# Cross-attention on array tiles: scores in 64x64 tiles over four banks, attention in 128x32 column tiles in one bank

## Chip, core and metric

The kernel runs on one core of one Trainium2 chip, in one launch. The metric is the device time of an execution in microseconds; the median of three executions before the change is 878.66 us (877.78 to 878.94).

## What is computed

One perceiver block over 32 sequences of 32 tokens, 512 wide, in three parts. Cut to what matters:

```
x = x + xattn(layernorm(x), ctx, ctx, mask)       # 16 heads of 32, 257 context rows per sequence
    Q = query @ Wq.T + bq;  K = key @ Wk.T + bk;  V = value @ Wv.T + bv
    scores  = einsum('bhqd,bhkd->bhqk', Q, K) / sqrt(32), masked
    attn    = einsum('bhqk,bhkd->bhqd', softmax(scores), V)
    return attn @ Wo.T + bo
x = x + fft_bind_attention(layernorm(x))          # rfft products, summed over the tokens, unbound
x = x + top1_moe(layernorm(x))                    # 8 experts 512 -> 2048 -> 512, gelu, the gate's expert alone
```

## The kernel before

Every product is made of float16 halves: an operand is split into a high and a low part, and three products (high x high, high x low, low x high) are added up in PSUM. ScalarE (ACT) writes the high part (`hi`, line 560), VectorE (DVE) the low one (`lo`, line 793). All engines run programs that are written out by hand in one order each and meet at semaphores; nothing is scheduled by a planner. The eight PSUM banks are BA to BH.

**Cross-attention, 16 steps of two sequences** (steps 2 to 13 in a loop of two). In step `st` PE makes four key projections `k_proj(c)` (12 matmuls of 512 columns each), the attention of step `st-1` for its two sequences, and four value projections `v_proj(t)` (12 of 512 each) with the step's scores between them. `scores(j)`, j = 4·sequence + chunk, handles four heads at once: the queries stand block-diagonally in `q_bd` (128 partitions = 4 heads of 32 dimensions, 128 columns = 4 heads of 32 queries, zeros off the diagonal), and three matmuls of 258 columns (257 keys and one for a bias) fill bank BC or BD in turn. `attention(b)` makes four products of seven matmuls, each 128 dimensions of v (4 heads) against 128 probability columns (4 heads of 32 queries); of the 128x128 result only the four diagonal 32x32 blocks are wanted, so `attention_hi` and `attention_lo` read them out of bank BG (BH for the second sequence) in four pieces of 32 partitions each.

DVE adds the mask to the scores (line 920, `scores`), takes the maxima (`maxima`), ACT the exponentials (`exp`, line 637), DVE the reciprocals, ACT and DVE the two halves of the probabilities (`p_hi`, `p_lo`, line 942). SP then has them transposed by DMA (`p_transposed`, line 341) into `pT`, which the next step's attention reads. GpSimd (POOL) prepares the last key (`last_keys`, lines 433 to 440), the last value row (line 448), and `q_bd` of the next step (line 458, four operations of 128x512; line 462 copies the keys' last column), and copies the attention's result out (line 468). The softmax of the second sequence reaches over the step's end: `exp(st-1, 1)`, `p_hi(st-1, 1)`, `p_lo(st-1, 1)` stand at the beginning of step `st`. ACT and DVE also split the next context block there (128x2048, `ctx_hl`). Steps 1, 14 and 15 carry the splitting of weights for the next part (`mixing_weights`), and a last step without projections folds them.

**Experts.** Eight experts run one after another. Each has eight weight pieces of 1 MB, which SP loads into four staging buffers `e_stage` (`load_piece`, line 363) as soon as DVE has split the piece that was there (`e_lo`). POOL fetches the tokens of the next expert with an indirect DMA (`gather_tokens`, line 518), PE transposes them (line 1560) after the first quarter of the second layer (line 1598).

## Time and profile before

| | |
|---|---|
| median of three executions | 878.66 us |
| the profiled execution's own time | 880.63 us |
| its span, first to last instruction | 878.7 us |
| PE busy | 823.2 us (94%) |
| DVE busy | 691.4 us (79%) |
| ACT busy | 495.3 us (56%) |
| POOL busy | 298.2 us (34%) |
| cross-attention steps | from some 44 to 485 us of the span |
| experts | from 645 us to the end |

The profile is of one execution. PE's busy time counts matmuls with modelled ends, so how fast PE really goes is read from how many matmuls of a shape start within a stretch. PEclk is the granted clock of TensorE, in tenths of full speed on the page, as a share in the views of stretches.

### The profile page before, as it was taken

The numbers are of one execution on the slowest core, as the hardware profiler recorded it, in microseconds if no ns is written. First come the engines' busy times: TensorE is split into PE (matmuls) and PEld (weight loads), VectorE is DVE, ScalarE is ACT, GpSimd is POOL, SyncE is SP. The second block draws the span as 40 slices with busy tenths as digits, with TensorE's granted clock in tenths as the row PEclk, the third lists the DMA queues.
The fourth block names the chain that finished last, engine by engine and source line by source line (L and its number), as shares of the span: only waits on it lengthen the run. The fifth ranks groups of instructions, "written<-read, shape, count | busy, mean of one in ns | idle before, by whom it ended". The sixth has DMA issues, their size and how long they took to land.

```text
span 878.7 us, 18573 instructions
## 1 busy us (share of the span) xinstructions
PE 823.2 (94%) x7168; PEld 563.3 (64%) x7168; DVE 691.4 (79%) x1069; ACT 495.3 (56%) x976; POOL 298.2 (34%) x322
## 2 busy tenths in 40 slices
PE   5979999999999999999998999997699999999994
PEld 2434555555555555555554844455599999999994
DVE  6967898888888878788887767788787797778850
ACT  3525546664556665556655603434587778777850
POOL 1365454433444423344443100003131422443222
PEclk9989999999999999999999999999599999999997
DMA  9431244322444322444213241111688988889811
GB/s 344 169 105 26 74 99 100 62 62 73 98 99 98 57 67 73 98 98 98 51 48 52 54 190 48 49 48 48 219 305 309 344 303 332 323 330 326 331 32 40
DMA packets 93150, 124.98 MB, mean 142 GB/s; under 512 B 75712, under 2 KB 78336, under 8 KB 81841
## 3 DMA queue, kind: packets, MB, share of 16 engines
q1 hardware_dynamic: 90528, 117.35, 42.3%
q0 software_dynamic: 2576, 7.02, 2.2%
q8 instruction: 29, 0.48, 0.2%
q14 instruction: 17, 0.13, 0.0%
HBM read 100.17 MB, written 6.88 MB: 122 GB/s over the span
## 4 chain that ended last, share of the span: by engine, by line
PE 75%; DVE 10%; ACT 6%; issue 5%; DMA 3%; POOL 1%; ACTq 0%; DVEq 0%; POOLq 0%
PE bank L1281 62%; PE bank L1598 10%; ACT arena L560 4%; DVE arena L793 3%; DVE arena L942 2%; DMA arena<-arena 2%; ACT arena L753 1%; DMA arena<-l_dram,arena 1%; DVE arena L808 1%; DVE arena L920 1%; PE bank L1560 1%; DVE arena L825 1%; DVE arena L926 1%; DMA arena<-in_x_t 0%; PE bank L1570 0%
## 5 line engine op out<-in xcount | busy, mean ns | idle before, releaser
L1281 PE MATMUL bank<-arena 128*128 128x512 f16 (+7 forms) x5296 | 684.6, 291 | 19.7 <-DMA arena<-arena 6.3
L1281 PEld LDWEIGHTS bank<-arena 128*128 128x128 f16 (+1 forms) x5296 | 430.4, 100 | 271.4 <-issue 14.3
L560 ACT ACTIVATE arena<-arena 128x256 f16<-128x256 f32 (+3 forms) x293 | 252.2, 905 | 19.5 <-DVE arena L937 7.5
L793 DVE SCALAR_TENSOR_TENSOR arena<-arena 128x2048 f16<-128x2048 f32 (+2 forms) x95 | 215.7, 2285 | 29.4 <-ACT arena L560 29.2
L560 ACT ACTIVATE arena<-bank 128x512 f16<-128x512 f32 (+2 forms) x319 | 134.6, 428 | 184.7 <-PE bank L1281 123.0
L793 DVE SCALAR_TENSOR_TENSOR arena<-bank,arena 128x512 f16<-128x512 f32 (+1 forms) x286 | 141.9, 505 | 55.2 <-ACT arena L560 50.6
L1598 PE MATMUL bank<-arena 128*128 128x160 f16 x1536 | 110.0, 233 | 0.6
L1598 PEld LDWEIGHTS bank<-arena 128*128 128x128 f16 x1536 | 106.1, 98 | 2.2 <-DVE arena L1217 1.8
L637 ACT ACTIVATE arena<-arena 128x257 f32<-128x257 f32 x128 | 63.5, 498 | 71.1 <-DVE arena L928 71.1
L510 POOL DMA_INDIRECT out<-arena x16 | 45.8, 2863 | 132.7 <-DVE arena L1212 130.2
L942 DVE SCALAR_TENSOR_TENSOR arena<-arena 128x256 f16<-128x256 f32 x128 | 84.5, 720 | 0.0
L458 POOL TENSOR_TENSOR arena<-arena 128x512 f16<-128x512 f32 (+1 forms) x64 | 71.1, 1130 | 0.3 <-POOL arena L417 0.2
L920 DVE SCALAR_TENSOR_TENSOR arena<-bank,arena 128x257 f32<-128x257 f32 x128 | 56.7, 484 | 4.8 <-PE bank L1281 4.2
L433 POOL TENSOR_TENSOR arena<-arena 128x4 f32<-128x4 f32 x32 | 6.4, 199 | 148.7 <-DVE arena L937 148.7
L1217 DVE SCALAR_TENSOR_TENSOR arena<-arena 128x320 f16<-128x320 f32 x64 | 29.4, 487 | 23.4 <-ACT arena L560 23.3
L468 POOL COPY arena<-arena 128x256 f16 (+1 forms) x32 | 14.6, 485 | 97.8 <-DVE arena L793 97.8
L402 POOL TENSOR_TENSOR arena<-arena 128x4 f32<-128x4 f32 (+1 forms) x7 | 6.5, 927 | 116.3 <-DVE arena L801 116.3
L753 ACT ACTIVATE arena<-bank 128x320 f32<-128x320 f32 x64 | 27.2, 425 | 26.8 <-PE bank L1281 26.8
L721 ACT ACTIVATE arena<-bank,arena 128x512 f32<-128x512 f32 x24 | 16.5, 686 | 45.3 <-PE bank L1281 44.9
L926 DVE TENSOR_REDUCE arena<-arena 128x4 f32<-128x1028 f32 x32 | 39.2, 1224 | 1.1
L462 POOL COPY arena<-arena 128x8 f16 (+1 forms) x32 | 39.7, 1240 | 0.0
L448 POOL TENSOR_TENSOR arena<-arena 32x1024 f16<-32x1024 f32 (+1 forms) x16 | 30.5, 1908 | 2.9 <-issue 2.1
(95 smaller groups left out, 346.2 us busy)
## 6 DMA issues: line engine op xcount, KB each, us to landing
arena<-in_w SPq DMA_DIRECT2D x64, 1024.0 KB, 5.5
arena<-in_ctx_t SPq DMA_DIRECT2D x16, 1024.0 KB, 5.1
arena<-in_awt SPq DMA_DIRECT2D x3, 1024.0 KB, 6.9
l_dram<-arena SPq DMA_DIRECT2D x4, 512.0 KB, 3.6
x_dram<-arena SPq DMA_DIRECT2D x1, 2048.0 KB, 12.9
arena<-in_x_t SPq DMA_DIRECT2D x2, 512.0 KB, 4.5
arena<-in_wq_t SPq DMA_DIRECT2D x1, 1024.0 KB, 6.8
arena<-in_x_t SPq DMA_DIRECT2D x1, 1024.0 KB, 8.9
```

What stands on the lines that cost most here:

```text
L458: g.tensor_tensor(q_bd[n][:, :, b, :].rearrange("p c (r q) -> p c r q", r=HC), qT[n][:, :, bass.ds(st * (PB * S) + b * S, S)].unsqueeze(2) ...
L462: last = g.tensor_copy(kT[n][:, :, :, LM], klast[n][:, :, bass.ds(st * PB, PB)])
L510: g.indirect_dma_start(out=out_rows, out_offset=bass.IndirectOffsetOnAxis(ap=ids[part][:, e, 1:2].bitcast(U32), axis=0), in_=y_rows[part], ...
L560: return a.activation(dst, src, ACT.Copy, scale=scale)
L637: a.activation(sm[:, j, :], sm[:, j, :], ACT.Exp, bias=neg_max[:, j:j + 1], scale=ISD / (SX * SK), accum_out=score_sums[:, j:j + 1]).then_ ...
L753: a.activation(hid_f[k % 4], H_BANKS[k % 4][:, 0:2 * CAP].rearrange("p (c x) -> p c x", c=2), ACT.Gelu_apprx_tanh, scale=1.0 / (SX * SG)). ...
L793: return v.scalar_tensor_tensor(dst, src, scale, h, ALU.mult, ALU.subtract)
L920: v.scalar_tensor_tensor(sm[:, j, :], bank[:, 0:L], bank[:, L:L + 1], mask_bias, ALU.add, ALU.add).then_inc(s["s_free"], 1)
L926: v.reduce_max(row_max[:, js], sm[:, js, :], AX_X).then_inc(s["s_max"], 1)
L942: v.scalar_tensor_tensor(p_hl[1][b][:, j - b * KC, :], sm[:, j, 0:LM], recip[:, j:j + 1], p_hl[0][b][:, j - b * KC, :], ALU.mult, ALU.subtract
L1281: last = m.matmul(out_ap, w, x, start=(n == 0), stop=(n == len(pairs) - 1))
L1598: last = m.matmul((BC, BD)[c % 2][:, 0:CAP], w[u][:, f, :], hid_hl[z][:, f, :], start=(f == 0 and u + z == 0), stop=(f == FC - 1 and u == 1))
```

## The change

1. **Scores.** `scores(b)` now makes the four chunks of a sequence, two at a time. Each chunk is cut into two halves of two heads: 64 partitions of keys and queries, 64 output rows (`q_bd` is half as wide). Three passes over four 64x64 tiles of the array (two chunks, two halves) go to two banks; the odd chunk's halves are swapped. Four banks (BC, BD, BF, BH) take a sequence's four chunks, so the projections keep three (BA, BB, BE) in place of four.
2. **Attention.** Per product there are now 7 x 4 matmuls: for each of the four heads its own 32 columns of v against its own 32 probability columns, in four column tiles (128 partitions by 32 columns) of the array. Only the wanted blocks are made, and both sequences stand side by side in 256 columns of bank BG, so `attention_hi` and `attention_lo` are one operation each.
3. **Order of a step.** PE: k_proj 0 to 3, attention of both sequences, scores of the first, v_proj 0 and 1, scores of the second, v_proj 2 and 3. ACT and DVE follow: the exponentials and the reciprocals of the second sequence are now in the step itself; POOL makes `q_bd` ahead of the last value row.
4. **Experts.** From the second expert on, each piece has a staging buffer of its own (eight, four of them where qT, wk and wv lay), and SP loads a piece as soon as its own buffer is free. The second expert's last four pieces wait for the stored layernorm and for `xs_done`, no longer for `e_lo`.

```diff
-        q_bd = [xa.take([KC, PB, P], F16) for _ in range(2)]
+        q_bd = [xa.take([KC, PB, HALF], F16) for _ in range(2)]
...
-        e_stage = [view((172 + 8 * n) * KB, [PW], F32) for n in range(4)]
+        e_stage = ([view((172 + 8 * n) * KB, [PW], F32) for n in range(4)]
+                   + [view(q_off + n * PIECE, [PW], F32) for n in range(4)])
+        assert q_off + 4 * PIECE <= wo_off
+
+        def is_first(n):
+
+            return isinstance(n, int) and n == 0
+
+        def piece_stage(n, k):
+
+            return k % 4 if is_first(n) else k
+
+        def piece_landed(n, k):
+
+            if is_first(n):
+                return 16 * (k // 4) + 16
+            return n * 16 + 32 if k < 4 else n * 16
         assert wo_off + 3 * PIECE <= dft_off and after_spec + PIECE <= 172 * KB
 
...
-            def load_piece(e, n, done):
-
-                sp.wait_ge(s["e_lo"], done)
-                src = i["w1"] if n < 4 else i["w2"]
-                sp.dma_start(e_stage[n % 4], src[bass.ds(e * 4 + n % 4, 1)].rearrange("a p x -> p (a x)")
-                             ).then_inc(s[f"e_landed{n % 4}"], 16)
+            def load_piece(n, e, k):
+
+                src = i["w1"] if k < 4 else i["w2"]
+                at = piece_stage(n, k)
+                sp.dma_start(e_stage[at], src[bass.ds(e * 4 + k % 4, 1)].rearrange("a p x -> p (a x)")
+                             ).then_inc(s[f"e_landed{at}"], 16)
...
             sp.wait_ge(s["pv_free"], STEPS * PB)
-            for n in range(PIECES - 1):
-                load_piece(0, n, from_zero(n - 3))
+            for k in range(PIECES - 1):
+                sp.wait_ge(s["e_lo"], from_zero(k - 3))
+                load_piece(0, 0, k)
...
             sp.wait_ge(s["x2_done"], NT)
             sp.dma_start(i["x2_dram"].rearrange("(t p) d -> p t d", p=P), x_tok).then_inc(s["x2_stored"], 16)
 
-            def rest_of_round(r):
-                with sp.Fori(1, E) as e:
-                    for n in range(PIECES):
-                        load_piece(e, n, r * (E * PIECES) + e * PIECES + (n - 3))
-
-            rest_of_round(0)
+            for k in range(PIECES):
+                if k < 4:
+                    sp.wait_ge(s["e_lo"], k + 5)
+                if k == 4:
+                    sp.wait_ge(s["l2_stored"], 64)
+                    sp.wait_ge(s["xs_done"], 2)
+                load_piece(1, 1, k)
+
+            def expert_pieces(n, e):
+
+                for k in range(PIECES):
+                    sp.wait_ge(s["e_lo"], n * PIECES + (k - 7))
+                    load_piece(n, e, k)
+
+            with sp.Fori(2, E) as e:
+                expert_pieces(e, e)
             sp.wait_ge(s["routed"], 1)
             with sp.If(sp.value_load(more_rounds[0:1, 0:1], min_val=0, max_val=1) > 0):
                 with sp.Fori(1, ROUNDS) as r:
-                    for n in range(PIECES):
-                        load_piece(0, n, r * (E * PIECES) + (n - 3))
-                    rest_of_round(r)
...
             def step(st, cur=True, prev=True):
                 if prev:
+                    last_keys(st - 1, 1)
+                if cur:
+                    pool.wait_ge(s["s_ps"], st * PAIRS)
+                    pool.sem_inc(s["pool_waits"], 1)
+                    for n in range(2):
+                        for b in range(PB):
+                            g.tensor_tensor(q_bd[n][:, :, b, :].rearrange("p c (r q) -> p c r q", r=2),
+                                            qT[n][:, :, bass.ds(st * (PB * S) + b * S, S)].unsqueeze(2)
+                                            .broadcast_to((P, KC, 2, S)),
+                                            own_head.unsqueeze(1).unsqueeze(3).broadcast_to((P, KC, 2, S)), ALU.mult)
+                        last = g.tensor_copy(kT[n][:, :, :, LM], klast[n][:, :, bass.ds(st * PB, PB)])
+                    last.then_inc(s["q_ready"], 1)
+                if prev:
                     pool.wait_ge(s["vl_landed"], 64)
                     pool.wait_ge(s["pv_ps"], from_zero(st * 2 - 2))
...
+                def attention_hi():
+
+                    act.wait_ge(s["pv_ps"], st * 2)
+                    hi(att_st[0], pv_rows, 1.0 / SP_).then_inc(s["pv_hi"], 1)
+
                 if prev:
                     p_hi(st - 1, 1)
+                k_hi(0)
                 k_hi(1)
                 if nxt:
...
-                if prev:
-                    attention_hi(1)
+                    attention_hi()
                 if mixing is not None:
                     mixing_weights_hi(mixing, 1)
+                v_hi(0)
+                if cur:
+                    exp(st, 0)
                 v_hi(1)
                 if cur:
-                    exp(st, 0)
+                    p_hi(st, 0)
                 v_hi(2)
                 if cur:
-                    p_hi(st, 0)
+                    exp(st, 1)
                 v_hi(3)
 
...
@@ -943,18 +972,11 @@
                                                p_hl[0][b][:, j - b * KC, :], ALU.mult, ALU.subtract
                                                ).then_inc(s["p_lo"], 1)
 
-                def attention_lo(b):
-
-                    dve.wait_ge(s["pv_hi"], st * 2 - 1 + b)
-                    for r in range(HC):
-                        rows = slice(r * DK, (r + 1) * DK)
-                        last = lo(att_st[1][rows, :, b, :],
-                                  (BG, BH)[b][rows, :].rearrange("p (c x) -> p c x", c=KC)[:, :, r * S:(r + 1) * S],
-                                  1.0 / SP_, att_st[0][rows, :, b, :])
-                    last.then_inc(s["pv_free"], 1)
-
-                if prev:
-                    reciprocals(st - 1, 1)
+                def attention_lo():
+
+                    dve.wait_ge(s["pv_hi"], st)
+                    lo(att_st[1], pv_rows, 1.0 / SP_, att_st[0]).then_inc(s["pv_free"], 2)
+
                 k_lo(0)
                 if prev:
...
-                    scores(0)
-                    scores(1)
+                    for j in range(KC):
+                        scores(j)
+                    maxima(0)
+                v_lo(0)
+                if cur:
+                    reciprocals(st, 0)
                 v_lo(1)
                 if cur:
-                    scores(2)
-                    scores(3)
-                    maxima(0)
-                    scores(4)
-                    scores(5)
-                    reciprocals(st, 0)
+                    for j in range(KC, PAIRS):
+                        scores(j)
+                    maxima(1)
                 v_lo(2)
                 if cur:
-                    scores(6)
-                    scores(7)
-                    maxima(1)
+                    p_lo(st, 0)
+                    reciprocals(st, 1)
                 v_lo(3)
-                if cur:
-                    p_lo(st, 0)
 
             step(0, 0, prev=False)
...
                 def k_proj(c):
                     if cur:
-                        pe.wait_ge(s["proj_free"], from_zero(n0 + c - 3))
-                        split_product(proj_banks[c][:], wk, ctx_hl[par],
+                        pe.wait_ge(s["proj_free"], from_zero(n0 + (-1, 0, -2, 1)[c]))
+                        split_product(proj_bank(c)[:], wk, ctx_hl[par],
                                       lambda k: (slice(None), k, slice(c * P, (c + 1) * P)),
                                       lambda k: (slice(None), k, slice(None))).then_inc(s["proj_ps"], 1)
                     else:
@@ -1366,8 +1383,8 @@
 
                 def v_proj(t):
                     if cur:
-                        pe.wait_ge(s["proj_free"], n0 + 1 + t)
-                        split_product(proj_banks[t][:], ctx_hl[par], wv,
+                        pe.wait_ge(s["proj_free"], n0 + 2 + t)
+                        split_product(proj_bank(KC + t)[:], ctx_hl[par], wv,
                                       lambda k: (slice(None), k, slice(t * P, (t + 1) * P)),
                                       lambda k: (slice(None), k, slice(None))).then_inc(s["proj_ps"], 1)
                     else:
@@ -1375,20 +1392,30 @@
 
                 def attention(b):
                     for c in range(KC):
-                        cols = slice(c * P, (c + 1) * P)
-                        j = b * KC + c
-                        pairs = [(v_hl[u][:, b * 2 + kt, cols], pT[b][:, (z * KC + c) * 2 + kt, :])
+                        pairs = [(v_hl[u][:, b * 2 + kt, c * P:(c + 1) * P], pT[b][:, (z * KC + c) * 2 + kt, :])
                                  for kt in range(2) for u, z in ((0, 0), (0, 1), (1, 0))]
-                        pairs.append((vl_cur[:, j, :], pT[b][:, P_BLOCKS - 1, :]))
-                        last = product((BG, BH)[b][:, cols], pairs)
+                        pairs.append((vl_cur[:, b * KC + c, :], pT[b][:, P_BLOCKS - 1, :]))
+                        cols = slice((c * PB + b) * S, (c * PB + b + 1) * S)
+                        for n, (w, x) in enumerate(pairs):
+                            for r in range(HC):
+                                own = slice(r * DK, (r + 1) * DK)
+                                at = (r + 2 * (c % 2)) % HC
+                                last = m.matmul(BG[own, cols], w[:, own], x[:, at * S:(at + 1) * S],
+                                                start=(n == 0), stop=(n == len(pairs) - 1))
                     last.then_inc(s["pv_ps"], 1)
 
-                def scores(j):
-                    b, c = divmod(j, KC)
-                    pe.wait_ge(s["s_free"], from_zero(n0 + j - 1))
-                    product((BC, BD)[j % 2][:, 0:L + 1],
-                            [(u[:, c, b, :], z[:, c, b, :]) for u, z in hl_passes(q_bd, kT)]
-                            ).then_inc(s["s_ps"], 1)
+                def scores(b):
+
+                    for c in range(0, KC, 2):
+                        pe.wait_ge(s["s_free"], from_zero(n0 + b * KC + c - 2))
+                        pe.sem_inc(s["pe_waits"], 1)
+                        tiles = [(c + odd, r, (r + odd) % 2) for odd in range(2) for r in range(2)]
+                        for n, (u, z) in enumerate(hl_passes(q_bd, kT)):
+                            for cc, r, at in tiles:
+                                rows = slice(r * HALF, (r + 1) * HALF)
+                                last = m.matmul(SCORE_BANKS[cc][at * HALF:(at + 1) * HALF, 0:L + 1], u[rows, cc, b, :],
+                                                z[rows, cc, b, :], start=(n == 0), stop=(n == 2))
+                        last.then_inc(s["s_ps"], 2)
 
                 if cur:
                     pe.wait_ge(s["split_lo"], st + 1)
...
                     pe.wait_ge(s["vl_ready"], st)
                     pe.wait_ge(s["pv_free"], from_zero(st * 2 - 2))
-                    pe.wait_ge(s["pt_landed0"], st * 16)
-                    attention(0)
-                v_proj(0)
-                if prev:
-                    pe.wait_ge(s["pt_landed1"], st * 16)
-                    attention(1)
+                    for b in range(PB):
+                        pe.wait_ge(s[f"pt_landed{b}"], st * 16)
+                        attention(b)
                 if cur:
                     pe.wait_ge(s["q_ready"], st + 1)
                     pe.wait_ge(s["proj_free"], n0 + 4)
                     scores(0)
-                    scores(1)
+                v_proj(0)
                 v_proj(1)
                 if cur:
-                    scores(2)
-                    scores(3)
+                    scores(1)
                 v_proj(2)
-                if cur:
-                    scores(4)
-                    scores(5)
                 v_proj(3)
-                if cur:
-                    scores(6)
-                    scores(7)
 
             step(0, 0, prev=False)
...
             step(STEPS, 0, cur=False)
             pe.wait_ge(s["ab_split"], 3)
-            pe.wait_ge(s["pv_free"], STEPS * PB - 1)
...
         "ident": np.eye(P, dtype=np.float32),
         "ident16": np.eye(P, dtype=np.float16),
-        "own_head": np.repeat(np.eye(HC, dtype=np.float32), DK, 0),
```

Not shown: replaced names (`proj_bank(c)` for `proj_banks[c]`, `piece_stage` in `piece_hi` and `piece_lo`), new semaphores, and the removed parts of POOL's step that stand earlier now.

How the instructions stand now. PE, middle of step 2 in the loop, before (128x512: projections, 128x128: attention, 128x258: scores; REGISTER_ALU and ISA rows set up semaphore waits):

```order
L1281 MATMUL bank<-arena 128x512 x24
L1403 ISA
L1404 REGISTER_ALU
L1281 MATMUL bank<-arena 128x128 x28
L1369 REGISTER_ALU
L1281 MATMUL bank<-arena 128x512 x12
L1281 MATMUL bank<-arena 128x128 x28
L1412 REGISTER_ALU
L1281 MATMUL bank<-arena 128x258 x6
```

and now (32x32: a column tile of the attention, 64x258: a tile of the scores):

```order
L1298 MATMUL bank<-arena 128x512 x12
L1430 ISA
L1432 REGISTER_ALU
L1403 MATMUL bank<-arena 32x32 x224
L1436 REGISTER_ALU
L1416 MATMUL bank<-arena 64x258 x24
L1386 REGISTER_ALU
L1298 MATMUL bank<-arena 128x512 x12
L1386 REGISTER_ALU
L1298 MATMUL bank<-arena 128x512 x12
L1416 MATMUL bank<-arena 64x258 x24
```

The two attentions have joined and grown from 28 to 112 matmuls each, and 24 matmuls of scores follow at once, where there were 6; the value projections all stand behind them.

DVE, the same step, from the split of the context block (128x2048) on, before (line 793 with 128x2x256: k_lo, with 32x4x32: attention_lo, with 128x512: v_lo; line 920: scores):

```order
L793 SCALAR_TENSOR_TENSOR arena<-arena 128x2048
L901 REGISTER_ALU
L793 SCALAR_TENSOR_TENSOR arena<-bank,arena 128x2x256
L948 ISA
L793 SCALAR_TENSOR_TENSOR arena<-bank,arena 32x4x32 x4
L910 REGISTER_ALU
L793 SCALAR_TENSOR_TENSOR arena<-bank,arena 128x512
L793 SCALAR_TENSOR_TENSOR arena<-bank,arena 32x4x32 x4
L920 SCALAR_TENSOR_TENSOR arena<-bank,arena 128x257 x2
L910 REGISTER_ALU
L793 SCALAR_TENSOR_TENSOR arena<-bank,arena 128x512
L920 SCALAR_TENSOR_TENSOR arena<-bank,arena 128x257 x2
```

and now (lines 822 and 949 are 793 and 920 of before, 128x256 is attention_lo, line 955 the maxima):

```order
L822 SCALAR_TENSOR_TENSOR arena<-arena 128x2048
L930 REGISTER_ALU
L822 SCALAR_TENSOR_TENSOR arena<-bank,arena 128x2x256
L822 SCALAR_TENSOR_TENSOR arena<-bank,arena 128x256
L997 REGISTER_ALU
L949 SCALAR_TENSOR_TENSOR arena<-bank,arena 128x257 x4
L955 TENSOR_REDUCE arena<-arena 128x4
L956 REGISTER_ALU
L957 TENSOR_SCALAR arena<-arena 128x4
```

Between the split and the scores stand one k_lo and one attention_lo; two attention_lo of four pieces each and a v_lo have gone from there.

## Rows read from the trace of the kernel before

**Rows 1.** Page, busy time and the span in 40 slices:

```profile
PE 823.2 (94%) x7168; PEld 563.3 (64%) x7168; DVE 691.4 (79%) x1069; ACT 495.3 (56%) x976; POOL 298.2 (34%) x322
...
PE   5979999999999999999998999997699999999994
...
PEclk9989999999999999999999999999599999999997
```

**Rows 2.** Waits of PE in 75 to 500 us: us in total, times, longest:

```profile
PE bank L1281 <- DMA arena<-arena: 6.3, 4, 2.3
PE bank L1281 <- DVE arena L920: 3.3, 4, 1.0
```

**Rows 3.** Timeline of POOL, last_keys of the second batch: start, us, idle before:

```profile
74.55 0.20 POOL L433 TENSOR_TENSOR arena<-arena 128x4 f32<-128x4 f32 x1 [14.97 <-DVE arena L937]
...
134.59 0.20 POOL L433 TENSOR_TENSOR arena<-arena 128x4 f32<-128x4 f32 x1 [6.22 <-DVE arena L937]
...
425.96 0.20 POOL L433 TENSOR_TENSOR arena<-arena 128x4 f32<-128x4 f32 x1 [6.22 <-DVE arena L937]
...
483.26 0.20 POOL L433 TENSOR_TENSOR arena<-arena 128x4 f32<-128x4 f32 x1 [5.89 <-DVE arena L937]
```

**Rows 4.** Groups by shape in 187.56 to 214.06 us, one step:

```profile
L1281 PE MATMUL bank<-arena 128*128 128x512 f16 x97 | 21.9, 379 | 0.0
...
L793 DVE SCALAR_TENSOR_TENSOR arena<-bank,arena 128x512 f16<-128x512 f32 x9 | 6.2, 687 | 1.6 <-ACT arena L560 1.3
...
L560 ACT ACTIVATE arena<-bank 128x512 f16<-128x512 f32 x8 | 4.7, 584 | 4.8 <-PE bank L1281 4.8
...
L920 DVE SCALAR_TENSOR_TENSOR arena<-bank,arena 128x257 f32<-128x257 f32 x8 | 3.5, 485 | 0.0
L1281 PE MATMUL bank<-arena 128*128 128x128 f16 x56 | 3.5, 219 | 0.0
L1281 PE MATMUL bank<-arena 128*128 128x258 f16 x24 | 3.3, 273 | 0.0
...
L793 DVE SCALAR_TENSOR_TENSOR arena<-bank,arena 32x128 f16<-32x128 f32 x8 | 2.3, 286 | 1.5 <-ACT arena L560 1.4
```

**Rows 5.** Timeline of PE, long runs of one shape (start, us, count):

```profile
545.37 14.84 PE L1281 MATMUL bank<-arena 128*128 128x512 f16 x68
...
655.43 0.91 PE L1560 MATMUL bank<-arena 128*128 128x128 f16 x16 [1.24 <-DMA arena<-l_dram,arena]
656.28 10.13 PE L1598 MATMUL bank<-arena 128*128 128x160 f16 x144
```

**Rows 6.** Timeline of PE, small and alternating products:

```profile
626.44 0.35 PE L1281 MATMUL bank<-arena 128*128 128x8 f16 x8
...
683.12 0.27 PE L1570 MATMUL bank<-arena 128*128 128x128 f32 x1
683.23 0.27 PE L1571 MATMUL bank<-arena 128*32 128x128 f32 x1
683.34 0.27 PE L1570 MATMUL bank<-arena 128*128 128x128 f32 x1
```

**Rows 7.** Timeline of DVE inside one step:

```profile
191.06 1.66 DVE L942 SCALAR_TENSOR_TENSOR arena<-arena 128x256 f16<-128x256 f32 x4
...
193.78 3.23 DVE L942 SCALAR_TENSOR_TENSOR arena<-arena 128x256 f16<-128x256 f32 x4
...
198.22 2.99 DVE L793 SCALAR_TENSOR_TENSOR arena<-arena 128x2048 f16<-128x2048 f32 x1
```

**Rows 8.** Timeline of SP in that step; issues of DMA, median us to landing:

```profile
192.74 6.81 SPq L341 DMA_TRANSPOSE arena<-arena  x2
...
arena<-arena SPq DMA_TRANSPOSE x32, 4.4
```

**Rows 9.** Stretches of the experts: busy us (count) of PE, PEld, DVE, ACT, POOL; PEclk, DMA share, GB/s:

```profile
650.00:655.00 5.00, 4.19 (x60) 3.90 (x57) 4.28 (x5) 4.94 (x7) 2.86 (x3) 1.00 0.93 292
684.00:712.50 28.50, 28.41 (x410) 28.01 (x408) 23.35 (x21) 22.04 (x29) 10.70 (x6) 1.00 0.88 321
```

67 lines of the change are left out of this document (25 added, 42 removed).

## The prediction, on record before the changed kernel was run

> **What bounds the kernel.** I read the page's shares first: PE is busy for 94% of the span at a granted clock of 0.9 or more nearly throughout, DVE for 79% [rows 1]. Then the waits of PE in the 425 us of cross-attention: less than 10 us in all, some of them for the transposes by DMA and some for DVE's reading of the scores [rows 2]. Then POOL's operation that marks each step: from the mark at 134.59 to that at 425.96 lie 11 steps of 26.49 us; steps 1 and 2 take 60.0 us together, the last two 57.3 us [rows 3]. Last, whether PE is full by its own pace and not only by modelled ends. Its long runs give the time from one start to the next: (14.84 - 0.38)/67 = 0.216 us for 512 columns, (10.13 - 0.23)/143 = 0.069 us for 160 [rows 5], which is N/2.4 ns plus some 2.5 ns. So 258 columns take 0.110 and 128 columns 0.056 us. A step has 96 matmuls of 512, 24 of 258 and 56 of 128 [rows 4]: 20.7 + 2.64 + 3.12 = 26.5 us, the measured step. **PE sets it alone**: whatever leaves PE shortens the step until another chain comes up. In the experts it is the same: 384 x 0.069 = 26.6, eight f32 transposes at 0.109 [rows 6], and 0.85 for the f16 ones and their surroundings [rows 5] are 28.3 of 28.5 us [rows 9].
>
> **Scores.** Out go 24 x 0.110 = 2.64 us a step; in come 48 tiles of 258 columns, 12 groups of four disjoint tiles. If the four run beside each other a group takes about the 0.110 us of one: 1.32 us, **a gain of 1.3 us**. No row shows two tiles at once, so bounds: each pair of weight load and matmul needs a slot of some 0.026 us (eight matmuls of 8 columns: (0.35 - 0.17)/7 = 0.026 us each [rows 6]), four are 0.104, still below 0.110; and without any overlap 48 x 0.110 = 5.28 us, a loss of 2.6. I take 1.32, since the slot fits.
>
> **Attention.** Out go 3.12 us; in come 224 pairs with 32 columns, 56 groups of four. Streaming them is nothing (0.013 us at N/2.4). Lower bound: a group costs one slot, 56 x 0.026 = 1.5 us. Upper bound: every pair costs a slot, 224 x 0.026 = 5.8 us. The point where attention is even is 3.12/224 = 0.014 us a pair. The 0.026 us were measured with each load and matmul in the same place of the array, where a load waits for the matmul before it; the change's four follow each other in different places, so I lean to the overlapped side and take 8 to 10 ns a pair, about 2.0 us. The Trainium skill (TensorEngine Tiling (Array Packing), Instruction Overhead) speaks against this change: each matmul has an overhead of about 60 cycles, and no tiling factor should be taken from a dimension that is already small. By it a pair of 32 columns costs what one of 60 does; the trace agrees for single places, and by that rule without overlap the attention would take 5.6 us, an estimate from the page's figure. The Trainium skill's page TensorE: Matmul & The Clock Gate (Measured speedup vs the span model) has tiles of 512 columns start about 4 ns apart, by which it would take some 1.5 us; no run here shows it.
>
> **Changes of tile shape.** The array now changes five times a step (128, 128x32, 64x64, 128, 64x64, 128). The nearest row: eight full f16 transposes and eight of 32 rows took 0.85 us from 655.43 to 656.28 [rows 5]; less 8 x 0.056 and 8 x 0.026 there are 0.2 us for two changes, so 0.1 each and 0.5 us a step. Alternating 128 and 32 columns in f32 every 0.11 us shows none [rows 6]: the other bound is 0.
>
> PE's own sum is then 20.7 + 1.3 + 2.0 + 0.5 = 24.5 us.
>
> **What comes up next.** Let T be the start of k_proj(0). `scores(0)` now stands right behind the attention and waits for the fourth k_lo. Down DVE: k_proj(0) ends at T+2.8, k_hi 0.6, k_lo 0.7 (rows of 128x512 [rows 4]): T+4.3 with the semaphores. Four p_lo, 3.2 us beside POOL's q_bd as now (1.7 without [rows 7]): T+7.5. k_lo(1), k_lo(2) (its projection ends at T+7.9): T+9.2. The split of the context block, 3.0 [rows 7]: T+12.2. k_lo(3): T+12.8. PE has done projections and attention at T+10.4+2.1 = T+12.5, so it waits until T+12.9. The transposes of the second sequence run into the same place: p_lo at T+7.5 plus 4.4 us to landing [rows 8] is T+11.9, when half of the attention is still to come. From T+12.9: 0.7 scores, 5.2 two v_proj, 0.7, 5.2 and four changes less the hidden one, 0.3: **T+24.9**. So the speed of the attention hardly matters below 1 us a sequence: the step goes from 26.5 to 24.9, **1.6 us**.
>
> DVE and ACT lose work: eight pieces of 0.29 become one of about 0.4, 1.9 us off DVE [rows 4], and as much off ACT; q_bd is half as long on POOL. DVE would have some 20 of 24.9 us, so none of these is a second term; they are why DVE is not yet the bound. POOL's moved value row is hidden (nobody waits for it until T+10.4), its q_bd is needed only at T+12.5. SP's queue has the same DMAs in the same order. The scores' waits for free banks cost nothing: four banks are read a half step earlier. Where only three projection banks are left, k_proj(0) waits for the v_lo of two before it, done by then.
>
> **Sum.** 15 intervals (11 of 26.49 and the four longer ones, in which DVE's extra work bounds and DVE is relieved by as much) x 1.6 = 24.0; the first step's scores 1.3; the last step's attention, waiting for its transposes, nothing. The experts: PE bounds them, so more staging buffers gain 0. But the second expert's last four pieces, 4 MB, are now asked for as soon as the first gather is done, at the moment when the gather of its tokens is in flight and PE already waits 1.24 us for it [rows 5], with the DMA engines at 0.93 [rows 9]. Bounds: 0, and 4 MB at 321 GB/s [rows 9] = 13 us if all of them went first. I take 1.5, about the present wait once more, since the gather shares the engines with other pieces already. Total 24.0 + 1.3 - 1.5 = 23.8 us off the profiled execution's 880.6, or off the median of 878.7, from which it stands 0.2%: **855 us**.
>
> **Rivals.**
> - *Chains loosen (0.12).* With q_bd half as long, p_lo may run at its 1.7 us and the split faster too. Then scores start at T+12.2 or sooner, and PE is bound by its own 23.9 to 24.3 with the lower bound of the attention: 15 x 2.5 = 37, **840 us**. For: DVE takes 1.66 or 3.23 us for the same four operations, by whether POOL works. Against: POOL's q_bd begins with the reciprocals, as now.
> - *Half overlap (0.20).* A pair of the attention costs 14 to 16 ns: 3.4 us. PE's sum 20.7 + 1.3 + 3.4 + 0.5 = 25.9, past the other chains: 0.6 us a step, 9 + 1.3 - 1.5: **870 us**.
> - *The slot is PE's, not the place's (0.15).* Every pair costs 0.026 us wherever it goes: attention 5.8 us, PE 28.3 us a step, 1.8 more than now: 15 x 1.8 - 1.3 + 1.5 = 27 us **slower, 906 us**. It decides from where 224 p + 1.3 + 0.5 = 3.12 + 2.64, p = 3.96/224 = 17.7 ns a pair. For: no row shows a pair in less than 26 ns. Against: the eight that show it follow one another in one place of the array. It is the Trainium skill's rule on overhead from above, taken as an issue limit.
> - *Tiles do not overlap at all (0.05).* 5.8 + 5.3 + 0.5 in place of 5.76 is 5.8 a step: 88 us slower, 966 us.
> - *Nothing gained (0.03).* p near 18 ns, or DVE's chain later than I have it: 877 to 880.
>
> **How the numbers follow.** My forecast has 0.45, between 848 and 862. A measurement of this kernel tells 0.2% (1.8 us) from no change. Faster: 0.45 + 0.12 + 0.20 = 0.77; same 0.03; slower 0.20. The range reaches from the loosened chains to the half overlap with its experts' stall and a pair at the even point: 838 to 885. The slower fifth stays outside.
>
> **What would show it.** A step of 24.9 us between POOL's marks; about 1.3 us for 48 score tiles and some 2 for 224 attention tiles; PE waiting in each step some tenths of a microsecond for DVE's fourth k_lo (line 822) or for the transposes; DVE at about 80% of a step; experts at 28.5 us each and a longer wait before the second one's transposes. Starts of the attention's matmuls 26 ns apart would make me wrong on the sign; a step of 24 us without waits would show that I placed the chains too late.

## The result, and the profile after

| | before | after |
|---|---|---|
| median of 12 runs | 878.86 us (877.78 to 880.77) | 875.38 us (871.85 to 878.03) |
| ratio | | 0.995, 95% interval 0.9937 to 0.9962 |
| profiled execution: time, span | 880.63, 878.7 us | 873.88, 872.1 us |
| granted clock, mean | 0.977 | 0.973 |

The kernel is 3.5 us faster where 23.8 were forecast: the sign held, the size did not. In the two profiled executions the gain is 6.7 us. Single executions stood far off, one of e4's ten (4548.66), one of e6's four (1057.14, at a granted clock of 0.747) and one of e13's six (892.59, at 0.927); the ratios below leave them out, the medians of these three runs do not.

The page of the changed kernel, to be read against [rows 1]: busy times, PE's slices, clock, instruction queue, chain.

```profile
PE 798.9 (92%) x10240; PEld 525.6 (60%) x10240; DVE 648.2 (74%) x957; ACT 470.7 (54%) x864; POOL 238.2 (27%) x322
...
PE   5979887999999999999999999996699999999994
...
PEclk9989999999999999999999999999699999999997
...
q8 instruction: 38, 0.62, 0.3%
...
PE 43%; DVE 20%; ACT 16%; issue 10%; DMA 9%; POOL 1%; DVEq 0%; ACTq 0%; POOLq 0%
```

PE has lost 24 us of work. All else got lighter too, yet PE's slices show 8, 8, 7 early in cross-attention, and the share of "issue" in the chain, time in which an engine waits for nothing that the profile shows, is 10% (5% before).

Waits of PE in 75 to 500 us, against [rows 2]:

```profile
PE bank L1403 <- DMA arena<-arena: 12.6, 15, 1.4
PE bank L1416 <- issue: 5.2, 2, 4.3
PE bank L1298 <- DVE arena L822: 4.7, 5, 1.5
PE bank L1403 <- issue: 4.1, 3, 2.1
```

The attention of the second sequence (L1403) now waits for its transposes, 15 times, once in every step but the last. And 9.3 us are waits for nothing that the profile names ("issue"): 5.2 ahead of scores or between them (L1416), 4.1 inside attentions (L1403). PE's timeline in a step of the loop:

```profile
201.82 1.06 PE L1403 MATMUL bank<-arena 128*32 128x32 f16 x112
203.56 1.06 PE L1403 MATMUL bank<-arena 128*32 128x32 f16 x112 [0.68 <-DMA arena<-arena]
204.63 0.85 PE L1416 MATMUL bank<-arena 64*64 64x258 f16 x24
205.41 5.35 PE L1298 MATMUL bank<-arena 128*128 128x512 f16 x24
```

The tiles do what was hoped. 24 score tiles take 205.41 - 204.63 = 0.78 us from their start to the next group's (forecast 0.66 and a switch). 112 attention products take 1.06 us. How fast they start is read from the same timeline when its window ends earlier (201.82:202.03, then 201.82:202.56):

```profile
201.82 0.38 PE L1403 MATMUL bank<-arena 128*32 128x32 f16 x32
201.82 0.92 PE L1403 MATMUL bank<-arena 128*32 128x32 f16 x95
```

The first 32 start within 0.21 us, 6.6 ns a pair; the 63 after them take 0.53 us, 8.4 ns a pair, some 33 ns for a group of four.

The marks on POOL that answer to [rows 3]:

```profile
135.77 0.20 POOL L467 TENSOR_TENSOR arena<-arena 128x4 f32<-128x4 f32 x1 [5.56 <-DVE arena L966]
...
167.17 0.20 POOL L467 TENSOR_TENSOR arena<-arena 128x4 f32<-128x4 f32 x1 [5.57 <-DVE arena L966]
...
420.87 0.20 POOL L467 TENSOR_TENSOR arena<-arena 128x4 f32<-128x4 f32 x1 [5.57 <-DVE arena L966]
```

From 167.17 to 420.87 lie ten steps of 25.37 us, against 26.49. But from 135.77 to 167.17 one step takes 31.4. PE's timeline says where, there and at the other stands:

```profile
90.69 0.90 PE L1403 MATMUL bank<-arena 128*32 128x32 f16 x93 [1.24 <-DMA arena<-arena]
92.85 0.30 PE L1403 MATMUL bank<-arena 128*32 128x32 f16 x19 [1.26 <-issue]
...
146.72 1.06 PE L1403 MATMUL bank<-arena 128*32 128x32 f16 x112 [0.64 <-DMA arena<-arena]
152.12 1.50 PE L1416 MATMUL bank<-arena 64*64 64x258 f16 x24 [4.34 <-issue]
153.56 6.50 PE L1298 MATMUL bank<-arena 128*128 128x512 f16 x24
159.99 0.85 PE L1416 MATMUL bank<-arena 64*64 64x258 f16 x24
...
432.89 0.49 PE L1416 MATMUL bank<-arena 64*64 64x258 f16 x9
434.26 0.65 PE L1416 MATMUL bank<-arena 64*64 64x258 f16 x15 [0.88 <-issue]
...
485.13 2.04 PE L1403 MATMUL bank<-arena 128*32 128x32 f16 x209
489.24 0.27 PE L1403 MATMUL bank<-arena 128*32 128x32 f16 x15 [2.06 <-issue]
```

Products whose data lie ready break off in the middle of an accumulation: after 93 of 112, after 9 of 24 tiles, after 209 of 224. (The longest stand is ahead of scores(0) of step 3; POOL had done its q_bd at 139.9 and DVE the fourth k_lo at 146.7.) These places are in steps 1, 2, 3 and 14 and in the last attention, behind step 15. Steps 2 and 3 are the first pass of PE's loop of twelve steps; the others are written out. In the five later passes no such stand occurs, and none in the kernel before. The packets of the instruction queue in the same trace (16,384 bytes each) say what goes before their ends (a stand goes here from the start of the last product to the start of the next):

```
PE stands          a fetch starts, lands     PE resumes after landing
 91.41 to  92.85    90.03      92.16          0.69
121.30 to 122.26   119.91     120.81          1.45
147.59 to 152.12   149.62     150.55          1.57
433.11 to 434.26   431.92     432.87          1.39
486.99 to 489.24   486.81     487.76          1.48
```

Between the packets of 153.63 and 424.35 this queue brings nothing: the loop's code is there. The queue has 38 packets in place of 29, and in 75 to 500 us 18 in place of 9. **Code that runs for the first time, with more instructions in less time, is not brought in time.** Why the fetch of step 3 starts 2 us after PE has stopped the trace leaves open; the DMA engines are full until 149.0 (share 1.02) with the context's load, whose last packet lands at 149.67.

The stand of step 3 has a second price. Stretches of PE: busy us (count), granted clock, DMA share, GB/s:

```profile
149.10:152.12 3.02, 0.00 (x0) 0.50 0.06 22
152.12:155.90 3.78, 3.78 (x30) 0.50 0.02 4
```

While PE stood, its granted clock fell to the lower of its two levels, 1.2 in place of 2.4 GHz, and stayed there for the first 3.8 us of work: 24 score tiles and 24 projection products take 1.44 + 6.43 us from start to start there, where at the full clock (204.63 to 210.70) they take 0.78 + 5.29. That is 1.8 us. Step 3 is then accounted for: 25.4 as a looped step, 4.3 standing, 1.8 at the lower clock make 31.5 us, and 31.4 were measured. The same happened behind the stand in the last attention: the clock is 0.50 from 490.4 to 493.8, with PE busy throughout, 1.7 us lost. In the kernel before it is at 1.00 from 96 to 610; its own two stretches at 0.50 (60.5 to 67.3 and 87.8 to 91.2) also follow waits of PE.

PE's long wait in the first step, [5.65 <-issue] ahead of scores(0) at 62.18, is another: PE stood there before as well (4.71 ahead of 62.44). It is for DVE's fourth k_lo, not for POOL's first q_bd, which was done at 50.6. POOL from there, and DVE:

```profile
50.49 8.84 POOL L512 TENSOR_TENSOR arena<-arena 128x4096 f32<-128x4096 f32 x1
...
55.22 6.26 DVE L822 SCALAR_TENSOR_TENSOR arena<-arena 128x2048 f16<-128x2048 f32 x1
61.40 0.68 DVE L822 SCALAR_TENSOR_TENSOR arena<-bank,arena 128x512 f16<-128x512 f32 x1
```

DVE's split of the context block, 2.28 us in the loop, takes 6.26 beside POOL's addition of the bias (L512) and ends 2.15 us after it, and the k_lo that scores(0) wait for stands behind it, done at 62.1. In the kernel before the split took 7.91, ending at 61.7. DVE in one looped step, against [rows 7]:

```profile
195.40 3.66 DVE L971 SCALAR_TENSOR_TENSOR arena<-arena 128x256 f16<-128x256 f32 x4
...
200.58 2.28 DVE L822 SCALAR_TENSOR_TENSOR arena<-arena 128x2048 f16<-128x2048 f32 x1
```

and the last of the four p_lo at 195.40 alone (window 197.1:198.5):

```profile
196.94 2.11 DVE L971 SCALAR_TENSOR_TENSOR arena<-arena 128x256 f16<-128x256 f32 x1
```

The second sequence's p_lo, on which its transposes hang, took 3.23 and now takes 3.66, since POOL does its q_bd (193.62 to 196.7) and then the value row (196.64 to 198.77) beside it. The value row alone makes most of it: the fourth p_lo, some 0.4 us by itself, starts 0.3 us behind it, takes 2.11 and ends 0.3 us after it. The split went from 2.99 to 2.28, free of POOL.

At the experts, the wait for the gather that was 1.24 in [rows 5]:

```profile
648.64 0.91 PE L1577 MATMUL bank<-arena 128*128 128x128 f16 x16 [2.13 <-DMA arena<-l_dram,arena]
```

### The profile page after: what moved, and what is told of

Read it like the earlier page. It is cut to its first block, busy times and chain, and to the rows that moved or that the text cites. A ratio compares the mean times of both kernels' runs of the same rounds, so it can differ in the third digit from the quotient of the medians.

```text
span 872.1 us, 24505 instructions
## 1 busy us (share of the span) xinstructions
PE 798.9 (92%) x10240; PEld 525.6 (60%) x10240; DVE 648.2 (74%) x957; ACT 470.7 (54%) x864; POOL 238.2 (27%) x322
## 4 chain that ended last, share of the span: by engine, by line
PE 43%; DVE 20%; ACT 16%; issue 10%; DMA 9%; POOL 1%; DVEq 0%; ACTq 0%; POOLq 0%
PE bank L1298 26%; PE bank L1615 10%; ACT arena L595 9%; DMA arena<-arena 8%; DVE arena L971 6%; DVE arena L949 5%; ACT arena L672 4%; DVE arena L955 4%; PE bank L1403 2%; DVE arena L822 2%; PE bank L1416 2%; ACT arena L782 1%; PE bank L1311 1%; DVE arena L957 1%; DMA arena<-l_dram,arena 1%
## 5 line engine op out<-in xcount | busy, mean ns | idle before, releaser
L1298 PE MATMUL bank<-arena 128*128 128x512 f16 (+7 forms) x4016 | 598.4, 310 | 8.6 <-DVE arena L822 4.7
L1298 PEld LDWEIGHTS bank<-arena 128*128 128x128 f16 (+2 forms) x4016 | 340.5, 100 | 254.8 <-issue 14.9
L595 ACT ACTIVATE arena<-bank 128x512 f16<-128x512 f32 (+3 forms) x207 | 108.0, 528 | 262.0 <-PE bank L1298 161.3
L822 DVE SCALAR_TENSOR_TENSOR arena<-arena 128x2048 f16<-128x2048 f32 (+2 forms) x95 | 203.9, 2160 | 32.0 <-ACT arena L595 31.9
L822 DVE SCALAR_TENSOR_TENSOR arena<-bank,arena 128x512 f16<-128x512 f32 (+1 forms) x174 | 113.2, 660 | 84.0 <-ACT arena L595 82.2
L949 DVE SCALAR_TENSOR_TENSOR arena<-bank,arena 128x257 f32<-128x257 f32 x128 | 53.5, 481 | 5.5 <-PE bank L1416 5.5
L1403 PE MATMUL bank<-arena 128*32 128x32 f16 x3584 | 34.8, 182 | 16.8 <-DMA arena<-arena 12.6
L1403 PEld LDWEIGHTS bank<-arena 128*32 128x32 f16 x3584 | 31.3, 93 | 25.3 <-DMA arena<-arena 14.1
L485 POOL TENSOR_TENSOR arena<-arena 128x256 f16<-128x256 f32 (+1 forms) x64 | 39.4, 636 | 1.4 <-POOL arena L451 0.2
```

The lines of the kernel that those rows point to most:

```text
L485: g.tensor_tensor(q_bd[n][:, :, b, :].rearrange("p c (r q) -> p c r q", r=2), qT[n][:, :, bass.ds(st * (PB * S) + b * S, S)].unsqueeze(2) ...
L595: return a.activation(dst, src, ACT.Copy, scale=scale)
L822: return v.scalar_tensor_tensor(dst, src, scale, h, ALU.mult, ALU.subtract)
L949: v.scalar_tensor_tensor(sm[:, j, :], bank[:, 0:L], bank[:, L:L + 1], mask_bias, ALU.add, ALU.add).then_inc(s["s_free"], 1)
L1298: last = m.matmul(out_ap, w, x, start=(n == 0), stop=(n == len(pairs) - 1))
L1403: last = m.matmul(BG[own, cols], w[:, own], x[:, at * S:(at + 1) * S], start=(n == 0), stop=(n == len(pairs) - 1))
```

## The experiments

All start from the changed kernel. Where the time of a step is given, it is the distance between the starts of two attentions in the loop: 26.49 before, 25.3 to 25.43 in the changed kernel. e1 to e8 had the kernel before at 878.8 to 879.2. But for e2 and e8, which leave work out or do other work, no ratio is 2% from 1, so small gains are read from the steps in the trace and the medians only checked against them.

**e1_split.** PE does attention(0), v_proj(0), attention(1), scores(0), v_proj(1).

```diff
-                    for b in range(PB):
-                        pe.wait_ge(s[f"pt_landed{b}"], st * 16)
-                        attention(b)
+                    pe.wait_ge(s["pt_landed0"], st * 16)
+                    attention(0)
+                v_proj(0)
+                if prev:
+                    pe.wait_ge(s["pt_landed1"], st * 16)
+                    attention(1)
...
                     scores(0)
-                v_proj(0)
```

> Edit: on PE alone the first value projection goes back between the two attentions: attention(0), v_proj(0), attention(1), scores(0), v_proj(1). In the changed kernel's trace a looped step is 25.4 us and attention(1) waits 0.7 to 0.8 us in each for its transposes by DMA; besides, PE stands still for want of instructions after some 410 to 450 dense small ones (4.3 us in step 3, 2.1 us in the last step, 0.8 to 1.3 us in three others). Theory A (both the transposes and the supply of instructions took the gain): the wait for the transposes goes, since they have 2.6 us more, and the supply catches up in v_proj(0): looped steps 24.6 us, the stalls of issue shorter by 5 us or more, time some 860 us. Theory B (only the transposes): steps 24.6 us, stalls of issue stay, 866 us. Rival (DVE's order bounds the step, whatever PE does): steps stay at 25.4 us, 875 us.

Measured: 883.79, ratio 1.0051 (1.0034 to 1.0069); steps of 26.5. The transposes' wait is gone, and PE waits in k_proj for DVE, 17 times:

```profile
PE bank L1298 <- DVE arena L822: 27.9, 17, 4.6
```

So hiding one wait only moved it. What k_proj(0) waits for is v_lo(2) of the step before, which frees its bank (DVE at 236.99 for 0.68, PE from 237.73): DVE's hand-written order takes all scores and maxima before v_lo(2), and the first scores now come 2.7 us later. Of the three expectations it is the rival on DVE's order that held, and the step even grew. The stands without a named cause shrank to 1.4 us: the attentions are 12 long products apart. This order of PE alone loses 8 us against the changed kernel.

**e2_few.** One of the seven products of each attention tile; six sevenths of the attention are left out.

```diff
+                        pairs = pairs[:1]
                         for n, (w, x) in enumerate(pairs):
```

> Leaves out six of the seven products of every attention (64 matmuls a step in place of 448 loads and matmuls), so its output is not the block's. PE does 1.2 us less a step. If the transposes set the step, looped steps stay at 25.3 to 25.4 us and PE only waits longer. If the supply of instructions is the other loss, all stalls of issue but the first vanish: time 875 less some 8 us, 867 us. If PE's own work set the step, steps would be 24.2 us and the time 857 us. If the stalls come from something else in the loop's first pass (the branch, a semaphore), the 4.3 us in step 3 stay: 872 us or more.

Measured: 857.44, ratio 0.9759 (0.9704 to 0.9814); steps of 24.5; waits of PE in 75 to 500 us:

```profile
PE bank L1404 <- DMA arena<-arena: 25.8, 16, 4.0
```

With almost no attention the step falls by 0.9 only, since PE then waits some 1.5 us for the transposes in each: this is where the other chain stands. And there is no "issue" row: with 32 attention products a step, not 224, the code comes in time. Against the changed kernel that is 18 us, of which 15 x 0.9 = 13.5 are steps; the stands that are gone (9.3) are more than the rest. The instruction queue has 29 packets again, as before the change.

**e3_outer.** The loop over the four column tiles stands outside that over the seven products, so seven products in a row use one tile.

```diff
-                        for n, (w, x) in enumerate(pairs):
-                            for r in range(HC):
+                        for r in range(HC):
+                            for n, (w, x) in enumerate(pairs):
```

> The same 224 matmuls of the attention, but the seven products of one column tile follow each other before the next tile comes (loops r and n exchanged). If four tiles run beside each other only because their instructions alternate, each pair now costs the 25 to 26 ns of one place: attention 5.6 us a step instead of 1.4, the step some 3.5 us longer (part hidden in the wait for the transposes), 28.9 us, and the time some 925 us. If the queue reorders enough to overlap tiles anyway, nothing changes: 875 us.

Measured: 881.09 (one run, span 879.3); steps of 25.9 to 26.1. PE's timeline:

```profile
228.47 3.47 PE L1403 MATMUL bank<-arena 128*32 128x32 f16 x224
231.88 0.85 PE L1416 MATMUL bank<-arena 64*64 64x258 f16 x24
```

(231.88 - 228.47)/224 = 15.2 ns a pair, in place of 2.02/224 = 9.0 (e5 below), both with ends and switches. The order of the tiles sets the pace. But it is well under the 0.026 us of [rows 6]: even so the pairs overlap in part, and the expected loss came out much too large.

**e4_qwait.** POOL's q_bd waits until DVE has done p_lo.

```diff
                     pool.wait_ge(s["s_ps"], st * PAIRS)
+                    if prev:
+                        pool.wait_ge(s["p_lo"], st * PAIRS)
```

> One added wait: POOL begins q_bd only when the four p_lo of the second sequence are done. In the changed kernel these four take 3.8 us while POOL works and the same four take 1.7 us while it does not. If POOL's work slows them and they set the transposes, p_lo falls to 1.7 us, the transposes start 2.1 us earlier, attention(1) waits no more, the looped step goes to 24.7 us and the time down by some 10 us: 865 us. If q_bd then comes too late (it is needed at about 12 us of the step) PE waits for it instead and the step stays at 25.4 or grows. If the slowness of p_lo has another cause, p_lo stays at 3.8 and the step grows by what q_bd is late.

Measured: 876.65, ratio 0.9982 (0.9951 to 1.0012); no gain. In 200 to 400 us, DVE's p_lo and its split:

```profile
L973 DVE SCALAR_TENSOR_TENSOR arena<-arena 128x256 f16<-128x256 f32 x64 | 26.6, 477 | 0.0
...
L824 DVE SCALAR_TENSOR_TENSOR arena<-arena 128x2048 f16<-128x2048 f32 x8 | 26.7, 3336 | 0.0
```

p_lo did fall to 0.48 each (0.73 in the changed kernel, both as means over the two sequences), but the value row, still behind q_bd, slid onto the split, which rose from 2.28 to 3.34, and delayed k_lo(3): "PE bank L1418 <- DVE arena L824: 7.2, 11, 0.7" in 75 to 500 us. Steps are 25.34. The contention moved from one chain to the other.

**e5_pool.** As e4, and POOL's value row goes back to where the kernel before had it, ahead of last_keys of the second sequence.

```diff
                 if prev:
+                    pool.wait_ge(s["vl_landed"], 64)
+                    pool.wait_ge(s["pv_ps"], from_zero(st * 2 - 2))
+                    pool.sem_inc(s["pool_waits"], 1)
+                    g.tensor_tensor(vl_cur[0:LAST_ROWS],
...
                     last_keys(st - 1, 1)
...
+                    if prev:
+                        pool.wait_ge(s["p_lo"], st * PAIRS)
```

Not shown: the same value row taken out behind q_bd.

> POOL alone: its value row (2.1 us) goes back ahead of last_keys and q_bd, to where it overlaps nothing of DVE's long operations, and q_bd waits for p_lo as in the run with the added wait. There the p_lo fell from 3.8 to 1.7 us, but the value row came 0.47 us late for the attention and the split of the context block grew from 2.3 to 3.3 us, so that the fourth k_lo came some 0.7 us late: the step stayed at 25.3. Theory (two chains on DVE, both lengthened by POOL's work beside it, hold the looped step above PE's own sum): now p_lo takes 1.7 and the split 2.3 us, neither the transposes nor k_lo are waited for, and the looped step is 24.6 us, time some 9 us below the changed kernel's 875.4, 866 us. If the step stays at 25.3, some third chain holds it and the theory falls.

Measured: 870.86, ratio 0.9913 (0.9883 to 0.9943), span 865.7; steps of 24.52. PE's timeline and its waits:

```profile
226.90 2.02 PE L1404 MATMUL bank<-arena 128*32 128x32 f16 x224
228.92 0.85 PE L1417 MATMUL bank<-arena 64*64 64x258 f16 x24
229.70 5.35 PE L1299 MATMUL bank<-arena 128*128 128x512 f16 x24
234.99 0.85 PE L1417 MATMUL bank<-arena 64*64 64x258 f16 x24
235.77 15.71 PE L1299 MATMUL bank<-arena 128*128 128x512 f16 x72
251.42 2.02 PE L1404 MATMUL bank<-arena 128*32 128x32 f16 x224
```

```profile
PE bank L1404 <- issue: 9.5, 3, 3.8
PE bank L1417 <- issue: 5.5, 3, 2.8
```

Both p_lo and the split are short, and PE no longer waits in a looped step. Its step is its own sum, from start to start: 2.02 + 0.78 + 5.29 + 0.78 + 15.65 = 24.52, what the prediction added up for PE. Ten steps gain 8.5 us, yet the kernel gains 4.5: the stands of first-run code grew from 9.3 to 15.0, and the two longest (3.8 and 3.7) were again followed by the lower clock (0.50 from 92.0 to 98.8 and 126.2 to 129.6). PE stops at the same instructions as in the changed kernel, with 19 products of the attention left in step 1, 9 in step 2 and 15 in the last. In step 1 it gets there 2.1 us earlier (89.3 against 91.4) and goes on 0.4 later (93.2 against 92.9). What had been a wait for transposes was cover for the fetch.

**e6_first.** In the first step v_proj(0) goes ahead of scores(0) again.

```diff
+                if not prev:
+                    v_proj(0)
                 if cur:
...
                     scores(0)
-                v_proj(0)
+                if prev:
+                    v_proj(0)
```

> PE's first step alone: v_proj(0) goes ahead of scores(0), as before the change. In the changed kernel PE stands for 5.65 us in front of the first scores, for the first q_bd of POOL, where before it stood 4.7 us after having done v_proj(0) too. If that reordering cost the first step's gain, the stand falls to some 3.1 us and the time by 2.6 us: 873 us. If the first q_bd is not what PE waits for, nothing changes.

Measured: 874.04, ratio 0.9904 (0.9868 to 0.9941). PE's timeline:

```profile
62.04 1.50 PE L1416 MATMUL bank<-arena 64*64 64x258 f16 x24 [3.03 <-issue]
```

The stand fell from 5.65 to 3.03, since v_proj(0) fills a part of it. Scores(0) start as late as ever, at 62.04, for k_lo behind the long split. So the first attention starts only 0.8 earlier (87.5 against 88.26), and the stands behind it are longer ("PE bank L1403 <- issue: 7.3, 3, 4.1"). Without the far-off execution its median is 872.72, 2.7 us below the changed kernel's, from three executions; the trace accounts for the 0.8.

**e7_loop.** PE's loop takes in steps 14 and 15, which were written out.

```diff
-            with pe.Fori(1, STEPS // 2 - 1) as k:
+            with pe.Fori(1, STEPS // 2) as k:
...
-            step(STEPS - 2, 0)
-            step(STEPS - 1, 1)
```

> PE's loop takes in steps 14 and 15, which stood behind it as straight code (the same work, 1472 fewer loads and matmuls in the program). If the stalls of issue come from fetching code that runs for the first time, the one of about 1.1 us in step 14 goes (steps 14 and 15 run code that is already there), while those of steps 1 to 3 and of the last step stay: 1 to 3 us off, 873 us. If code is fetched anew in each pass, nothing changes, 875 us.

Measured: 873.2, ratio 0.9932 (0.9912 to 0.9953). The same operations, only run from code that is there:

```profile
429.80 1.06 PE L1403 MATMUL bank<-arena 128*32 128x32 f16 x112 [0.63 <-DMA arena<-arena]
430.86 0.85 PE L1416 MATMUL bank<-arena 64*64 64x258 f16 x24
```

The stand of step 14 is gone, and between the packets of 151.63 and 475.23 the instruction queue brings nothing (six from 424 to 464 in the changed kernel; 32 packets in all for 38). Those of steps 1, 2 and 3 stay (0.8, 1.2 and 4.2), and that of the last attention, 2.4, whose code stands behind the loop. This shows the supply of code as the cause, not the place in the data flow. The 2.2 us of the median are not clear of noise.

**e8_full.** Attention as 56 untiled products of 128 columns, scores as changed. The rows of the two sequences then overwrite each other, the output is another, and the experts' routing takes more rounds: of its 2412.82 us nothing can be read, of its cross-attention all.

> Undoes the attention's tiles alone on PE: 56 matmuls of 128x128 by 128 columns a step, as before, in place of 224 tiles. Both sequences write the same bank and the blocks that are read are no longer the right ones, so the output is not the block's; the readers' work is as in the changed kernel. PE: 20.7 + 3.1 + 1.6 = 25.4 to 25.6 us a step and 336 fewer loads and matmuls. If the supply of instructions cost what I read from the trace (some 9 us over the kernel), the looped steps are 26.0 us or a little less (the second attention, 0.7 us longer, stands in the transposes' cycle), all stalls of issue but the first vanish, and the time is about as the changed kernel's or better: 871 us. If the stalls stay, the time is 881 us. If dense instructions had cost nothing and tiles all, 885 us.

Measured: steps of 25.9, and waits of PE in 75 to 500 us:

```profile
PE bank L1298 <- DVE arena L822: 5.7, 4, 2.8
PE bank L1298 <- DMA arena<-arena: 5.2, 4, 2.5
```

From 26.49 to 25.9 is what the scores' tiles and the new order give by themselves, 0.6 for a forecast of 1.3 less switches, and from 25.9 to 24.5 is the attention's share once no other chain holds it. And no "issue" row: the stands come with the 168 more attention products a step. They are 336 more instructions a step, loads and matmuls.

**e9_all, e10_ffn, e11_asis, e12_ffn, e13_all.** These five had the kernel before at 890.8 us (e9, e10) and 890.5 us (e11 to e13, on another chip), 12 more than all others; the chip of e9 and e10 had had it at 879.2 for e5 to e8. e10 and e12 put the experts' staging buffers back (four pieces an expert); e9 and e13 are that with e5, e6 and e7 together; e11 is the changed kernel itself.

```diff
-            return k % 4 if is_first(n) else k
+            return k % 4
...
-            if is_first(n):
-                return 16 * (k // 4) + 16
-            return n * 16 + 32 if k < 4 else n * 16
+            return n * 32 + (16 * (k // 4) + 16)
```

Not shown: SP's waits, which go with the buffers. The changed kernel has its eight buffers from the second expert on, not for the first, as the text of e10 has it.

> The changed kernel with four edits at once: POOL makes the value row right after the waits of the step and its q_bd only behind p_lo(0) and p_lo(1) (as in e5_pool), v_proj(0) stands ahead of scores(0) in the first step alone (e6_first), PE's loop takes in the last two steps (e7_loop), and the experts' staging buffers are those of the kernel before. If the terms are separate, the gains add to the 875.4 of the changed kernel: -4.5 (e5_pool) -1.3 (e6_first) -2.2 (e7_loop) -0.9 (staging: the gather stall of 2.1 against 1.2) = 866.5, range 864 to 869; looped steps 24.5; the stalls of PE with nothing to wait for stay only where code runs for the first time (steps 0 to 3). Rival: those stalls are a supply of instructions that falls further behind the faster PE gets, so that what one edit gains the next stall takes: then about 870, no better than e5_pool alone, with the stalls of the first steps over 10 us in sum.

> The changed kernel with only the experts' staging buffers as in the kernel before (four for every expert, instead of eight for the first). If those buffers cost what the rows say, the wait of the gather's products for their data goes from 2.13 back to 1.24 and the kernel gains 0.9: 874.5. Rival: the gather's wait is set by how early the experts' loads are given and not by the buffers: then 875.4, wait about 2.1 as now. A third: the eight buffers do help the first expert, and the kernel is slower by the 0.5 or so that this is worth.

> The changed kernel itself, with no edit, so that the two kernels after it have their own base on the same chip (with e9_all and e10_ffn the kernel before took 890.8, where every other run had it at 878.8 to 879.2, and both had 11 to 14 waits of PE with nothing to wait for, 6.7 us in all, among the experts' products, which neither the kernel before nor the changed kernel had in their profiles). If those waits belong to the chip's state then and not to the staging buffers: ratio to before 0.995 as measured first, 874 to 876 where before takes 879, and no such waits; in a state with before at 890 again, the ratio still about 0.99 and the waits there too, in this kernel as well.

> The edit of e10_ffn once more (the experts' staging buffers of the kernel before), beside the changed kernel itself. If the waits among the experts' products seen in e10_ffn were the chip's: none here unless e11_asis has them too, and the time 0.5 to 1.0 below e11_asis (the gather's wait 0.6 to 1.2 in place of 2.1). If they were the staging's: this kernel has them and e11_asis has not, and it is 5 or so slower than e11_asis.

> The four edits of e9_all once more, beside the changed kernel itself. Terms that add: 866.5 where before takes 879 (0.986 of before, 9 below e11_asis). Stalls of supply that take back what the other edits give: about 870, no better than e5_pool alone (0.991). If the staging buffers of the kernel before cause the waits among the experts: about 871 or more, and those waits in this profile and not in e11_asis.

| run | us | ratio to before (95%) |
|---|---|---|
| e9_all | 873.81 | 0.9805 (0.9784 to 0.9826) |
| e13_all | 874.76 | 0.9824 (0.9801 to 0.9846) |
| e10_ffn | 882.0 | 0.9897 (0.9877 to 0.9917) |
| e12_ffn | 881.75 | 0.9899 (0.9879 to 0.9919) |
| e11_asis | 885.66 | 0.9934 (0.9916 to 0.9952) |

Waits of PE over the whole span, e11 and then e12:

```profile
PE bank L1298 <- issue: 6.7, 12, 1.0
...
PE bank L1577 <- DMA arena<-l_dram,arena: 2.3, 1, 2.3
```

```profile
PE bank L1292 <- issue: 6.9, 12, 1.0
...
PE bank L1571 <- DMA arena<-l_dram,arena: 0.8, 1, 0.8
```

The unedited kernel has the waits among the experts' products too, so they belong to that session and not to the staging buffers. They are not stands of first-run code: in e11 no packet of the instruction queue falls between 692 and 850 us, where most of them lie. What they are stays open. Between e11 and the two with the old staging the gather's wait differs by 1.5 to 1.7 us and the medians by 3.7 to 3.9; 2.0 to 2.7 us more lie ahead of the last attention, where no edit was (it starts at 487.17 against 485.17 and 484.43). Against e10, e11 had a stretch more at the lower clock there (121.8 to 125.1 at 0.50, PE busy in 3.05), which costs 1.5; the rest stays open. The three edits of e5, e6 and e7 are taken like for like, with the old staging on both sides: e9 is 8.2 us below e10 and e13 7.0 below e12, where 4.5 + 1.3 + 2.2 = 8.0 were expected. **The terms add, and e9_all beats both kernels**, by 1.8% to 2.0% of before, where 1.4% was expected (0.986). The expected rival was half right: the first-run stands did grow, to 12.2 us in e9 within 75 to 500 us, but they did not take the gain back.

## Why the prediction was right or wrong

*PE's own sum: right.* 24.5 us were added up for PE; e5 and e9, in which nothing else holds PE, have steps of 24.52. By terms: projections 20.94 for 20.7, scores 1.56 for 1.3, attention 2.02 for 2.0; the changes of tile shape stand in these and come to some 0.4 for 0.5.

*Scores: nearly right.* 0.78 us from start to start for 24 tiles, 1.56 a step with a switch in each, for 1.32 and a share of the 0.5 for switches.

*Attention: right, in part by luck.* Forecast 2.0 us for 224 pairs, measured 2.02. The "8 to 10 ns a pair" was a choice between bounds that no row gave. The lower bound, one slot of 26 ns for a group of four, was not reached: past the first eight groups a pair starts every 8.4 ns, 33 ns for four. The rule of the Trainium skill (TensorEngine Tiling (Array Packing), Instruction Overhead) against small dimensions would have given 5.6 us, an estimate from the page's figure; this case's trace does not agree with it for tiles in four different places. The rival "slot is PE's" falls with it.

*Next chain: named, but the wrong one of two held, 0.5 us out.* The step was forecast at 24.9 by DVE's fourth k_lo (T+12.8) with the transposes close behind; measured 25.4, by the transposes. With T = 191.4 and 216.7 in the timelines, p_lo ended at T+7.7 (forecast T+7.5), and the second attention, 1.06 us long, could start at T+12.2 to T+12.3 only, so that scores(0) started at T+13.2 to T+13.4 in place of T+12.9; the fourth k_lo was done at T+12.1. The step of the prediction that failed is "four p_lo, 3.2 us beside POOL's q_bd as now", with "POOL's moved value row is hidden (nobody waits for it until T+10.4)": nobody waits for it, but it works beside p_lo and holds up the fourth (3.66 to 3.77 in all). The split, costed at 3.0, took 2.28. In ten steps this is 4.7 us. e4 and e5 show it: without POOL beside p_lo and the split the looped step is 24.52, so the rival "Chains loosen" had the mechanism, but it needed another edit.

*Intervals of first-run code: wrong, and the largest error.* "15 intervals x 1.6" treated all steps alike. The step from the first attention of the loop's second half on (step 3) took 31.4 in place of 24.9: 6.5 us short by itself, 4.3 of it standing for code, 1.8 the lower clock behind that and 0.5 the chain. No term of the sum, and no rival, had the supply of instructions or a fall of the clock in it, though the order printed for PE had 192 more products a step. e2, e7 and e8 show the supply; the clock's share is read from the trace alone, as no experiment was made on it. With the 4.7 us of the ten steps this is 11.2 of the 13.2 us missing; the other 2 lie in the four intervals of steps 1, 2, 14 and 15, three of which have stands of 0.8 to 1.3. All 15 intervals gained 407.68 - 396.87 = 10.8 us for 24.0.

*First step: wrong by 1.5.* The 1.3 us for its scores were lost, since the new order puts scores(0), which wait for DVE's fourth k_lo behind the split that POOL's bias addition holds up, ahead of v_proj(0), which had filled part of that wait (62.18 against 62.44). That it was POOL's first q_bd, as I had taken it in e6, is wrong: q_bd was done at 50.6. The prediction checked this order only for steps in the loop.

*Last step and experts.* Forecast 0 and -1.5, measured -4.0 from the last attention's start to the end: 2.1 a stand for code inside that attention, 1.7 the lower clock behind it, 0.9 the gather (1.5 to 1.7 in the later session: the 1.5 was about right), less the 1.1 that the last attention is shorter by; 0.4 are not attributed.

The shortfalls 24.0 - 10.8 = 13.2, then 1.5 and 2.5, make 17 us, and 23.8 - 17 is the 6.7 of the two profiled executions. That the medians differ by only 3.5 is in the spread: the profiled run of before lay 1.8 above its median, that of the changed kernel 1.5 below, and the changed kernel's runs spread over 6 us, before's over 3.

## What to carry to other kernels

Where a change multiplies the instructions of a stretch and shortens it, add the supply of code to the sum: count the instructions of code that runs for the first time (written-out steps, a loop's first pass) apart from looped code, and keep such steps in the loop. Look at the granted clock behind every stand of some microseconds. Where an operation is moved on GpSimd "because nobody waits for it", look which VectorE operation it will then run beside. And check a new order in the first and last step separately, where the waits lie elsewhere.

## What the runs showed of the hardware

- Column tiles of 128x32 in four different places of the array: the first 32 pairs start 6.6 ns apart, all later ones 8.4 ns. Seven in a row in one place (e3): 15 ns a pair, where 8-column products in one untiled place took 26 ns.
- Stands of 0.8 to 4.3 us in the middle of ready products, each ended 0.7 to 1.6 us after a 16 KB fetch of instructions had landed; none in the loop's later passes. Making PE faster (e5) made them longer, 9.3 to 15.0 us in all, long products in between (e1) shortened them to 1.4, and fewer products (e2, e8) took them away.
- The granted clock fell to 0.50 while PE stood for 4.3 us and stayed there for 3.8 us of work, which cost 1.8 us more; behind a stand of 2.1 us it was at 0.50 for 3.4 us.
- Four VectorE operations on 128x256 in the arena: 1.66 us alone, 3.66 to 3.77 beside GpSimd's; one on 128x2048: 2.28 alone, 3.34 beside GpSimd's value row, 6.26 beside its 8.84 us addition, ending 2.15 us after that. Moving the GpSimd work only moved the cost, until it found a stretch with neither (e5).
- The kernel before took 890.5 to 890.8 us in a later session against 878.8 to 879.2, on one chip that had shown both, and the changed kernel 885.66 against 875.38, with 12 short waits of PE among the experts' products that it had not shown before; the ratios taken side by side were 0.995 and 0.9934.
